# Transposed, mean-centred x for a cross-attention block: read from DRAM in a second layout instead of transposed on TensorE

## The chip, the cores and the metric

The kernel runs on one core of one Trainium2 chip, as a single launch. The metric is device time in microseconds (us) of one execution; several executions are timed and the median is given. The profile is one further execution taken by the hardware profiler. Engines are named as in the profile: PE is TensorE's matmul side, PEld its weight loads, DVE is VectorE, ACT is ScalarE, POOL is GpSimd, SP is SyncE, which here issues nearly all DMAs.

## The reference, cut to what matters

```python
def _layernorm(x, axis=-1, eps=1e-05):
    m = jnp.mean(x, axis=axis, keepdims=True)
    v = jnp.var(x, axis=axis, keepdims=True)
    return (x - m) / jnp.sqrt(v + eps)
...
# x (8, 128, 512), ctx_4096 (8, 128, 512), 32 heads of 128, 8 KV heads
q = (query @ Wq).reshape(nb, q_len, H, D).transpose(0, 2, 1, 3)
k = (key @ Wk).reshape(nb, q_len, KVH, D).transpose(0, 2, 1, 3)
v = (value @ Wv).reshape(nb, q_len, KVH, D).transpose(0, 2, 1, 3)
q = q * cos + _rotate_half(q) * sin
k = k * cos + _rotate_half(k) * sin
scores = jnp.einsum('bhqd,bhkd->bhqk', q, k) / jnp.sqrt(jnp.float32(D))
scores = jnp.where(mask == 0, jnp.float32(-1000000000.0), scores)
attn = jax.nn.softmax(scores, axis=-1)
...
x = x + _L0_xattn_ref(_layernorm(x, axis=-1), ctx_4096, ctx_4096, pos_BxS2, mask_BxSxS2_ik0, ...)
x = x + _L0_ffn_ref(_layernorm(x, axis=-1), ...)
```

The query of the attention is the layer norm of x. Each row of x is centred and multiplied by one number, 1/sqrt(var + eps). The projection by Wq and the rotation are linear, so that number can be applied before the projection or to the row's scores. The router block behind it is not touched by the change.

## The kernel before, in words

Five instruction streams are written out by hand, one for each engine, each in the fixed order of the code. They meet only through semaphores: an instruction waits until a semaphore has reached a count, and whatever is written behind it on its engine waits with it. There are 1024 rows of x and of the context (8 batches of 128), 512 columns, 8 KV heads. Every fp32 product is made of three products of split operands: a tensor is copied by ACT to a rounded part (names with `_hi`) and DVE or POOL subtracts that from the original to get the rest (`_lo`).

The stages, in the order in which PE works through them:

- Values, 16 tiles (i = 0 to 15; U_V + i in the code): PE projects the context by Wv into four PSUM banks in turn (bank_a, bank_b, outp0, bank_c). `copy_values(i)`, on DVE for i < 10 and on ACT for i from 10 on, copies tile i to `v_stage` (6 slots); SP stores it to DRAM (`store_v(i)`). PE needs the copy of tile u - 4 before it starts tile u. `copy_values(i)` for i >= 6 needs the store of tile i - 6 to have landed.
- Around tiles 8 to 11 the layer-normed x is made: `normalise_x(j)` on DVE, four 128x128 transposes on PE in `transpose_x(j)`, `copy_x(j)` on ACT into `x_raw`. Each of the eight j is one batch; with four of them half of the columns (q = 0) are ready, with eight the other half (q = 1).
- POOL then makes four sums of the blocks of `x_raw` (`sum_x(0)`, `sum_x(1)`: four instructions each, for a Strassen-like product of seven block products). ACT rounds all seven blocks (`hi_x(i, q)`, three of them from `x_raw` as it stands, four from the sums) and DVE makes the rests (`lo_x(i, q)`). I call this the x chain. Interleaved with it on ACT are `copy_values(10)` to `copy_values(15)` and `hi_wk(0)` to `hi_wk(5)`, and on DVE `lo_wk(0)` to `lo_wk(5)`; SP loads wk tile r + 2 when `lo_wk(r)` is done.
- Keys, 16 tiles (k = 0 to 15): PE projects the context by Wk; ACT copies the swapped halves, POOL multiplies by sin, DVE by cos and adds. Key tile k needs the copy of the tile four before it, so tile 2 needs `copy_values(14)` and tile 3 `copy_values(15)`.
- Then the first queries, and the main loop over KV heads and batches (scores, softmax, values, output projection, with the next queries in between), and the router block.

SP's DMAs all go to one hardware queue, in the order of its code.

Of the kernel before, what the change touches and what calls it, by code (L numbers as in the profile page):

```python
# [18 lines left out]
F32 = mybir.dt.float32  # L19
# [13 lines left out]
SCALE = float(D) ** -0.5  # L33


# [29 lines left out]
X_AFTER = 8  # L65
X_ORDER = 0, 4, 1, 5, 2, 6, 3, 7
# [15 lines left out]
def xattn_ffn(nc, x, ctx, pos, mask, rope, wq, wk, wv, wo, router, router_bias, expert_bias, out):  # L82
    v_dram = nc.dram_tensor("v_dram", (KV * NH * P, HB * D), F32, kind="Internal").ap()
    k_dram = nc.dram_tensor("k_dram", (KV * P, T), F32, kind="Internal").ap()
    with ExitStack() as stack:
# [20 lines left out]
        kT = at("kT", [T], F32, 82)  # L106
        hold = at("hold", [5, W], F32, 86)
# [72 lines left out]
        x_norm = at("x_norm", [2, E], F32, 194)  # L180
# [11 lines left out]
        x_rstd = at("x_rstd", [B], F32, 206.90625)  # L192
# [28 lines left out]
        x_bank = [probT, attnT]  # L221
# [28 lines left out]
        rstd_done = sem("rstd_done")  # L250
        norm_done = sem("norm_done")
# [6 lines left out]
        x_ps = sem("x_ps")  # L258
        x_copied = sem("x_copied")
# [137 lines left out]
        def _(sp):  # L397
# [35 lines left out]

            v_tiles = v_dram.rearrange("(g n p) (b d) -> n b p g d", g=KV, n=NH, d=D)
# [45 lines left out]
            sp.wait_ge(x_ps, B)  # L480
# [57 lines left out]
        def _(pool):  # L538
# [66 lines left out]
            pool.tensor_tensor(x_rstd[:, :], x_var[:, :], power[:, :], ALU.pow).then_inc(rstd_done, 1)  # L605
# [18 lines left out]
            pool.wait_ge(mask_done, 1)  # L624
            sum_x(0)
# [194 lines left out]
        def _(act):  # L820
# [90 lines left out]
            def copy_x(j):  # L911
                act.wait_ge(x_ps, j + 1)
                b = X_ORDER[j]
                half, rows = b // HB, slice(b % HB * S, (b % HB + 1) * S)
                act.activation(x_raw[:, 2 * half:2 * half + 2, :, rows],
                               x_bank[j % 2][:, :].rearrange("p (a c k) -> p a c k", a=2, c=HALVES), ACT.Copy).then_inc(x_copied, 1)
# [28 lines left out]
            copy_x(0)  # L945
            copy_x(1)
# [4 lines left out]
            copy_x(2)  # L951
            copy_x(3)
            for i in (B11, B21, B22):
                hi_x(i, 0)
            copy_x(4)
            copy_x(5)
# [3 lines left out]
            copy_x(6)  # L960
            copy_x(7)
# [284 lines left out]
        def _(dve):  # L1246
# [38 lines left out]
            def normalise_x(j):  # L1285

                b = X_ORDER[j]
                if j >= 2:
                    dve.wait_ge(x_ps, j - 1)
                dve.tensor_scalar(x_norm[:, j % 2, :], resid[:, b, :], x_mv[:, b, 0:1], x_rstd[:, b:b + 1],  # L1290
                                  ALU.subtract, ALU.mult).then_inc(norm_done, 1)
# [17 lines left out]
            for i in range(V_ACT):  # L1309
                copy_values(i)  # L1310
                if i in (3, 5):
                    half = 0 if i == 3 else 1
                    dve.wait_ge(dma_x[half], 16)
                    for b in range(half * HB, (half + 1) * HB):
                        dve.bn_stats(x_stats[:, b, :], resid[:, b, :]).then_inc(x_counted, 1)
                if i == 5:
                    dve.wait_ge(x_counted, B)
                    for b in range(B):
                        dve.bn_aggr(x_mv[:, b, :], x_stats[:, b, :]).then_inc(x_averaged, 1)
                    dve.wait_ge(x_averaged, B)  # L1320
                    dve.tensor_scalar(x_var[:, :], x_mv[:, :, 1], EPS, None, ALU.add).then_inc(var_done, 1)
# [898 lines left out]
```

## Time and profile before

| | before |
|---|---|
| median of 3 runs | 585.93 us (585.85 to 588.29) |
| span of the profiled execution | 584.1 us |
| PE busy | 577.0 us, 99% of the span |
| DVE / ACT / POOL busy | 471.4 / 404.1 / 430.9 us |
| DMA moved | 45.39 MB |

The profiled execution's span runs from its first instruction to its last. Its own time is that span and what lies around it, about 1.8 us by the median of the runs (585.93 - 584.1). Times inside the profile count from the start of the span. In a row of a timeline the first number is the start, the second the time for the xN instructions in it, and a bracket names the idle time ahead and what ended it.

### The profile page before, as it was taken

The numbers are of one execution on the slowest core, as the hardware profiler recorded it, in microseconds if no ns is written. First come the engines' busy times: TensorE is split into PE (matmuls) and PEld (weight loads), VectorE is DVE, ScalarE is ACT, GpSimd is POOL, SyncE is SP. The second block draws the span as 40 slices with busy tenths as digits, with TensorE's granted clock in tenths as the row PEclk, the third lists the DMA queues.
The fourth block names the chain that finished last, engine by engine and source line by source line (L and its number), as shares of the span: only waits on it lengthen the run. The fifth ranks groups of instructions, "written<-read, shape, count | busy, mean of one in ns | idle before, by whom it ended". The sixth has DMA issues, their size and how long they took to land.

```text
span 584.1 us, 10617 instructions
## 1 busy us (share of the span) xinstructions
PE 577.0 (99%) x2999; PEld 489.5 (84%) x2999; DVE 471.4 (81%) x764; ACT 404.1 (69%) x1074; POOL 430.9 (74%) x404
## 2 busy tenths in 40 slices
PE   9999999999999999999999999999999999999997
PEld 7888888877888888888888888888888888888885
DVE  5779797799888779777987798779877986797986
ACT  6267654797777777777776777677776776586655
POOL 5477699698976878687868886888678865446554
PEclk9999999999999999999999999999999999999999
DMA  8963526112301310121012110311122011100002
GB/s 287 378 182 91 160 93 227 38 38 90 109 20 54 91 56 19 55 90 54 24 48 90 54 49 23 90 54 54 36 72 63 8 50 59 36 20 2 19 37 91
DMA packets 30960, 45.39 MB, mean 78 GB/s; under 512 B 3024, under 2 KB 11600, under 8 KB 30928
## 3 DMA queue, kind: packets, MB, share of 16 engines
q1 hardware_dynamic: 30112, 43.56, 23.4%
q0 software_dynamic: 384, 1.05, 0.5%
q10 hardware_dynamic: 432, 0.40, 0.2%
q8 instruction: 15, 0.25, 0.2%
q14 instruction: 17, 0.14, 0.1%
HBM read 35.03 MB, written 9.96 MB: 77 GB/s over the span
## 4 chain that ended last, share of the span: by engine, by line
PE 92%; DVE 3%; ACT 2%; issue 2%; POOL 1%; DVEq 0%; ACTq 0%
PE score L1885 9%; PE outp L1909 9%; PE outp L1913 9%; PE outp L1917 8%; PE bank_a L1757 5%; PE bank_a L1759 5%; PE bank_a L1758 5%; PE probT L1964 4%; PE attnT L1743 2%; PE attnT L1744 2%; PE attnT L1745 2%; PE bank_c L1759 2%; PE bank_c L1758 2%; PE bank_c L1757 2%; PE bank_a L1743 1%
## 5 line engine op out<-in xcount | busy, mean ns | idle before, releaser
L543 POOL TENSOR_TENSOR rot<-rot,sinT 128x512 f32<-128x512 f32 x75 | 103.1, 1375 | 44.9 <-ACT rot L827 44.9
L1002 ACT ACTIVATE probs<-score,negmax 128x128 f32<-128x128 f32 x256 | 90.7, 366 | 28.7 <-DVE negmax L1412 28.7
L661 POOL TENSOR_TENSOR probs<-probs,rsum 128x512 f32<-128x512 f32 x62 | 67.3, 1085 | 44.1 <-DVE rsum L1418 44.1
L1909 PE MATMUL outp<-wo_hi,oT_hi 128*128 128x512 f32 x240 | 94.9, 397 | 0.2 <-DVE wo_lo L1479 0.2
L1913 PE MATMUL outp<-wo_lo,oT_hi 128*128 128x512 f32 x240 | 93.4, 391 | 0.3 <-POOL wo_lo L548 0.3
L1917 PE MATMUL outp<-wo_hi,oT_lo 128*128 128x512 f32 x240 | 83.4, 389 | 0.0
L1425 DVE TENSOR_TENSOR resid<-resid,outp 128x512 f32<-128x512 f32 x60 | 41.0, 683 | 48.8 <-PE outp L1917 46.9
L1885 PEld LDWEIGHTS score<-kT,qT 128*128 128x128 f32 x512 | 66.8, 191 | 5.0
L1254 DVE TENSOR_TENSOR qT<-qT,rot 128x512 f32<-128x512 f32 x57 | 68.5, 1205 | 2.9 <-POOL rot L543 0.5
L1129 ACT ACTIVATE oT_hi<-attnT 128x512 fp32r<-128x512 f32 x64 | 38.1, 595 | 42.9 <-PE attnT L1745 41.7
L1011 ACT ACTIVATE pT_hi<-probT 128x512 fp32r<-128x512 f32 x64 | 38.4, 600 | 42.4 <-PE probT L1964 41.8
L1885 PE MATMUL score<-kT,qT 128*128 128x128 f32 x512 | 67.4, 274 | 0.0
L1437 DVE TENSOR_TENSOR oT_lo<-attnT,oT_hi 128x512 fp32r<-128x512 f32 x64 | 44.2, 690 | 14.4 <-ACT oT_hi L1129 14.4
L548 POOL TENSOR_TENSOR wo_lo<-ring_b,wo_hi 128x512 fp32r<-128x512 f32 x30 | 38.7, 1322 | 21.6 <-ACT wo_hi L885 21.6
L1909 PEld LDWEIGHTS outp<-wo_hi,oT_hi 128*128 128x128 f32 x240 | 45.0, 188 | 10.4 <-DVE wo_lo L1479 1.1
L1917 PEld LDWEIGHTS outp<-wo_hi,oT_lo 128*128 128x128 f32 x240 | 45.1, 188 | 10.0
L1913 PEld LDWEIGHTS outp<-wo_lo,oT_hi 128*128 128x128 f32 x240 | 45.1, 188 | 9.9 <-POOL wo_lo L548 0.7
L1757 PE MATMUL bank_a<-x_hi,w_hi 128*128 128x512 f32 x120 | 51.9, 432 | 0.0
L1002 ACT ACTIVATION_READ_ACCUMULATOR probs<-score,negmax 128x1 f32 x256 | 51.9, 203 | 0.0
L1404 DVE SCALAR_TENSOR_TENSOR score<-score,mask_bias 128x512 f32<-128x512 f32 x64 | 44.5, 695 | 6.3 <-PE score L1885 3.0
L1759 PE MATMUL bank_a<-x_hi,w_lo 128*128 128x512 f32 x120 | 47.3, 394 | 0.0
L1758 PE MATMUL bank_a<-x_lo,w_hi 128*128 128x512 f32 x120 | 47.0, 391 | 0.0
(366 smaller groups left out, 1531.0 us busy)
## 6 DMA issues: line engine op xcount, KB each, us to landing
ring_b<-in_wo SPq DMA_DIRECT2D x32, 256.0 KB, 3.0
ring_a<-in_wq SPq DMA_DIRECT2D x28, 256.0 KB, 2.8
v_dram<-v_stage SPq DMA_DIRECT2D x16, 256.0 KB, 4.2
v_raw<-v_dram SPq DMA_DIRECT2D x16, 256.0 KB, 2.6
k_dram<-k_stage SPq DMA_DIRECT2D x14, 256.0 KB, 2.1
kT<-k_dram SPq DMA_DIRECT2D x14, 256.0 KB, 2.7
ctx_in<-in_ctx SPq DMA_DIRECT2D x8, 256.0 KB, 6.4
ring_b<-in_wv SPq DMA_DIRECT2D x8, 256.0 KB, 8.0
```

What stands on the lines that cost most here:

```text
L543: pool.tensor_tensor(rot_of(k0), rot_of(k0), sinT[:, half * W:(half + 1) * W], ALU.mult).then_inc(sin_done, 1)
L661: pool.tensor_tensor(probs[:, p], probs[:, p], rsum[:, p, :].unsqueeze(2).broadcast_to([P, GH, S]), ALU.mult).then_inc(soft_done, 1)
L1002: last = act.activation(probs[:, p, h, :], heads(score[p][:, :])[:, h, :], ACT.Exp, bias=negmax[:, p, h:h + 1], accum_out=sums[:, p, h:h + 1])
L1254: dve.tensor_tensor(dst, src, rot_of(k), ALU.add).then_inc(rope_done, 1)
L1404: dve.scalar_tensor_tensor(heads(score[p][:, :]), heads(score[p][:, :]), SCALE, mask_bias[:, b, :].unsqueeze(1).broadcast_to([P, GH, S]), ...
L1757: pe.matmul(ps[:, :], w[0], m[0], start=start and c == 0, stop=False, skip_group_check=True)
L1758: pe.matmul(ps[:, :], w[0], m[1], start=False, stop=False, skip_group_check=True)
L1759: last = pe.matmul(ps[:, :], w[1], m[0], start=False, stop=stop and c == HALVES - 1, skip_group_check=True)
L1885: last = pe.matmul(score[p][:, h * S:(h + 1) * S], qT[:, half, h, b % HB * S:(b % HB + 1) * S], kT[:, b * S:(b + 1) * S], start=True, stop ...
L1909: pe.matmul(ps[:, :], oT_hi[:, cols], wo_hi[:, h, :], start=h == 0, stop=False)
L1913: return pe.matmul(ps[:, :], oT_hi[:, cols], wo_lo[:, h, :], start=False, stop=stop)
L1917: return pe.matmul(ps[:, :], oT_lo[:, cols], wo_hi[:, h, :], start=False, stop=stop)
```

## The change

Four things change, all in the first stage.

1. The kernel gets a second input, `xt`, x laid out with the 512 columns as rows. SP loads it straight into `x_raw` in four DMAs of 512 KB. The 32 transposes of `transpose_x`, the eight `copy_x` and the eight `normalise_x` go.
2. The means lie one to a partition, but in `x_raw` they must lie along the free axis. SP writes them to DRAM (`store_mean(half)`: 512 elements of 4 bytes, one element to a run) and reads them back into all 128 partitions (`load_mean(half)`: 256 KB into `x_mean`). DVE subtracts them in place in `centre_x(q, half)`, four instructions of 128x1024. `x_mean` lies where kT is written later.
3. 1/sqrt(var + eps) is made together with 1/sqrt(128) as `score_scale`, and the instruction that scales and masks the scores takes it as a scalar for each partition instead of a constant.
4. The mask's load moves ahead of the wk loads, and the wait for `x_ps` ahead of the first wo loads goes.

```diff
             load_x(1)
+            sp.dma_start(mask_in[:, :, :], mask).then_inc(dma_mask, 16)
+            load_xt(0)
+            load_xt(1)
             for r in range(RA):
                 load_wk(r)
-            sp.dma_start(mask_in[:, :, :], mask).then_inc(dma_mask, 16)
             for i in range(KB * B):
+                if i == 6:
+                    store_mean(1)
                 store_v(i)
+                if i == 3:
+                    store_mean(0)
+                if i == 5:
+                    load_mean(0)
+                if i == 7:
+                    load_mean(1)
...
+            def load_xt(half):
+                cols = slice(half * W, (half + 1) * W)
+                for a in range(2):
+                    sp.dma_start(x_raw[:, 2 * half + a, :, :],
+                                 xt[a * HE:(a + 1) * HE, cols].rearrange("(c p) k -> p c k", p=P)).then_inc(dma_xt[half], 16)
+            def store_mean(half):
+                sp.wait_ge(x_averaged, (half + 1) * HB)
+                row = mean_dram[0, half * W:(half + 1) * W].rearrange("(b s) -> s b", s=S)
+                sp.dma_start(row, x_mv[:, half * HB:(half + 1) * HB, 0],
+                             allow_slow_non_contiguous=True).then_inc(dma_mout[half], 16)
+            def load_mean(half):
+                cols = slice(half * W, (half + 1) * W)
+                sp.wait_ge(dma_mout[half], 16)
+                sp.dma_start(x_mean[:, cols], mean_dram[:, cols].broadcast_to([P, W])).then_inc(dma_mean[half], 16)
...
+            def centre_x(q, half):
+                if q == 0:
+                    dve.wait_ge(dma_xt[half], 32)
+                    dve.wait_ge(dma_mean[half], 16)
+                rows = slice(q * 2 * S, (q + 1) * 2 * S)
+                block = x_raw[:, 2 * half:2 * half + 2, :, rows].rearrange("p a c k -> p (a c) k")
+                mean = x_mean[:, half * W + q * 2 * S:half * W + (q + 1) * 2 * S].unsqueeze(1).broadcast_to([P, 2 * HALVES, 2 * S])
+                dve.tensor_tensor(block, block, mean, ALU.subtract).then_inc(x_centred, 1)
...
-                if i == X_AFTER - 1:
-                    dve.wait_ge(rstd_done, 1)
-                    dve.wait_ge(b_lo, KB * C)
-                if i >= X_AFTER - 1:
-                    normalise_x(2 * (i - X_AFTER + 1))
-                    normalise_x(2 * (i - X_AFTER + 1) + 1)
+                if i == 7:
+                    centre_x(0, 0)
+                if i == 8:
+                    centre_x(0, 1)
+            centre_x(1, 0)
+            centre_x(1, 1)
             lo_wk(0)
-            normalise_x(6)
-            normalise_x(7)
...
             def sum_x(q):
-                pool.wait_ge(x_copied, (q + 1) * HB)
+                pool.wait_ge(x_centred, NH * (q + 1))
...
             def hi_x(i, q):
-                    act.wait_ge(x_copied, (q + 1) * HB)
+                    act.wait_ge(x_centred, NH * (q + 1))
...
             def mask_scores(p, b, count):
-                dve.scalar_tensor_tensor(heads(score[p][:, :]), heads(score[p][:, :]), SCALE,
+                dve.scalar_tensor_tensor(heads(score[p][:, :]), heads(score[p][:, :]), score_scale[:, b:b + 1],
...
-                if X_AFTER <= i < X_AFTER + HB:
-                    transpose_x(2 * (i - X_AFTER))
-                    transpose_x(2 * (i - X_AFTER) + 1)
```

SP's stream from the second load of x to the eighth value store, before (resid is x by rows, early_pair are the first Wq tiles):

```order
L432 DMA resid<-in_x 128x4x512
L406 DMA ring_a<-in_wk 128x512 x2
L468 DMA mask_in<-in_mask 128x1024
L439 DMA v_dram<-v_stage 128x4x128 [waits proj_free] x3
L417 DMA early_pair_61<-in_wq 128x512 x2
L439 DMA v_dram<-v_stage 128x4x128 [waits proj_free] x4
L417 DMA early_pair_60<-in_wq 128x512 [waits b_lo]
L417 DMA early_pair_60<-in_wq 128x512
L439 DMA v_dram<-v_stage 128x4x128 [waits proj_free] x3
```

The same stretch of SP's stream in the changed kernel:

```order
L428 DMA resid<-in_x 128x4x512
L480 DMA mask_in<-in_mask 128x1024
L433 DMA x_raw<-in_xt 128x2x512 x4
L402 DMA ring_a<-in_wk 128x512 x2
L453 DMA v_dram<-v_stage 128x4x128 [waits proj_free] x3
L413 DMA early_pair_62<-in_wq 128x512 x2
L453 DMA v_dram<-v_stage 128x4x128 [waits proj_free]
L440 DMA mean_dram<-x_mv 128x4x1 [waits x_averaged]
L453 DMA v_dram<-v_stage 128x4x128 [waits proj_free] x2
L446 DMA x_mean<-mean_dram 128x512 [waits dma_mout0]
L440 DMA mean_dram<-x_mv 128x4x1 [waits x_averaged]
L453 DMA v_dram<-v_stage 128x4x128 [waits proj_free]
```

Four 512 KB loads now stand ahead of the wk loads and all value stores. Two waits for a mean to have landed in DRAM stand in the stream, the first shown here, and the second mean's store stands behind the first wait.

DVE's stream from value tile 6 on, before:

```order
L1283 COPY v_stage<-outp 128x512 [waits dma_vout0,proj_done]
L1324 TENSOR_SCALAR mask_bias<-mask_in 128x1024 [waits dma_mask]
L1283 COPY v_stage<-bank_c 128x512 [waits dma_vout1,proj_done]
L1290 TENSOR_SCALAR x_norm<-resid,x_mv,x_rstd 128x512 [waits b_lo,rstd_done]
L1290 TENSOR_SCALAR x_norm<-resid,x_mv,x_rstd 128x512
L1283 COPY v_stage<-bank_a 128x512 [waits dma_vout2,proj_done]
L1290 TENSOR_SCALAR x_norm<-resid,x_mv,x_rstd 128x512 [waits x_ps] x2
L1283 COPY v_stage<-bank_b 128x512 [waits dma_vout3,proj_done]
L1290 TENSOR_SCALAR x_norm<-resid,x_mv,x_rstd 128x512 [waits x_ps] x2
```

The same stretch of DVE's stream in the changed kernel:

```order
L1292 COPY v_stage<-outp 128x512 [waits dma_vout0,proj_done]
L1335 TENSOR_SCALAR mask_bias<-mask_in 128x1024 [waits dma_mask]
L1292 COPY v_stage<-bank_c 128x512 [waits dma_vout1,proj_done]
L1302 TENSOR_TENSOR x_raw<-x_raw,x_mean 128x4x256 [waits dma_mean0,dma_xt0]
L1292 COPY v_stage<-bank_a 128x512 [waits dma_vout2,proj_done]
L1302 TENSOR_TENSOR x_raw<-x_raw,x_mean 128x4x256 [waits dma_mean1,dma_xt1]
L1292 COPY v_stage<-bank_b 128x512 [waits dma_vout3,proj_done]
L1302 TENSOR_TENSOR x_raw<-x_raw,x_mean 128x4x256 x2
L1306 TENSOR_TENSOR wk_lo<-ring_a,wk_hi 128x512 [waits k_hi] x2
```

The copies of value tiles 8 and 9 now stand behind waits for DMAs, where they stood behind work of PE.

## Rows read from the trace of the kernel before

**Rows 1.** The page: span, busy time by engine, 40 slices.
```profile
span 584.1 us, 10617 instructions
PE 577.0 (99%) x2999; PEld 489.5 (84%) x2999; DVE 471.4 (81%) x764; ACT 404.1 (69%) x1074; POOL 430.9 (74%) x404
...
DMA  8963526112301310121012110311122011100002
```

**Rows 2.** Timeline of PE: value tiles and transposes, then key tiles.
```profile
30.39 0.47 PE L1743 MATMUL bank_a<-wv_hi,ctxT_hi 128*128 128x512 f32 x1
...
33.24 0.60 PE L1844 MATMUL probT<-ident,x_norm 128*128 128x128 f32 x4
...
44.91 0.47 PE L1743 MATMUL bank_a<-wv_hi,ctxT_hi 128*128 128x512 f32 x1
...
47.76 0.39 PE L1743 MATMUL bank_b<-wv_hi,ctxT_hi 128*128 128x512 f32 x1
...
50.48 0.39 PE L1743 MATMUL outp<-wv_hi,ctxT_hi 128*128 128x512 f32 x1
...
64.08 0.39 PE L1743 MATMUL bank_c<-ctxT_hi,wk_hi 128*128 128x512 f32 x1
```

**Rows 3.** DMA by windows 23:30, 17:23 and 26.3:27; issues: KB, us to landing.
```profile
DMA packets 2869, 2.62 MB, mean 374 GB/s; under 512 B 142, under 2 KB 2253, under 8 KB 2868
...
v_dram<-v_stage SPq DMA_DIRECT2D x3, 256.0 KB, 11.0
...
v_dram<-v_stage SPq DMA_DIRECT2D x1, 256.0 KB, 5.8
```

**Rows 4.** Timeline of SP: when the DMAs were issued.
```profile
17.61 0.40 SPq L439 DMA_DIRECT2D v_dram<-v_stage  x1
...
26.36 0.98 SPq L439 DMA_DIRECT2D v_dram<-v_stage  x1
```

**Rows 5.** DMA issues up to 110 us: KB each, median us to landing.
```profile
ring_a<-in_wk SPq DMA_DIRECT2D x8, 256.0 KB, 2.9
...
rbias<-in_router_bias SPq DMA_DIRECT2D x1, 32.0 KB, 4.4
pos_in<-in_pos ACTq DMA_DIRECT2D x1, 4.0 KB, 2.9
```

**Rows 6.** Timeline of DVE.
```profile
28.80 0.69 DVE L1283 COPY v_stage<-outp 128x512 f32<-128x512 f32 x1
...
37.67 1.45 DVE L1290 TENSOR_SCALAR x_norm<-resid,x_mv,x_rstd 128x512 f32<-128x512 f32 x2
39.03 1.78 DVE L1295 TENSOR_TENSOR wk_lo<-ring_a,wk_hi 128x512 fp32r<-128x512 f32 x1
41.14 2.54 DVE L1290 TENSOR_SCALAR x_norm<-resid,x_mv,x_rstd 128x512 f32<-128x512 f32 x2 [0.33 <-PE probT L1844]
...
60.91 0.68 DVE L1295 TENSOR_TENSOR wk_lo<-ring_a,wk_hi 128x512 fp32r<-128x512 f32 x1
```

**Rows 7.** Timeline of ACT.
```profile
37.99 0.59 ACT L915 ACTIVATE x_raw<-attnT 128x512 f32<-128x512 f32 x1
...
55.06 2.20 ACT L925 ACTIVATE x_hi<-x_raw 128x512 fp32r<-128x512 f32 x4 [3.08 <-POOL x_raw L621]
...
57.68 0.58 ACT L942 ACTIVATE v_stage<-outp 128x512 f32<-128x512 f32 x1
60.17 0.63 ACT L909 ACTIVATE wk_hi<-ring_a 128x512 fp32r<-128x512 f32 x1 [1.91 <-DMA ring_a<-in_wk]
60.71 0.58 ACT L942 ACTIVATE v_stage<-bank_c 128x512 f32<-128x512 f32 x1
```

**Rows 8.** Timeline of POOL.
```profile
38.79 1.48 POOL L616 TENSOR_TENSOR x_raw<-x_raw 128x512 f32<-128x512 f32 x1
```

**Rows 9.** The page's costliest groups (busy us, mean ns), and one line's instructions (ns min/median/max).
```profile
L1404 DVE SCALAR_TENSOR_TENSOR score<-score,mask_bias 128x512 f32<-128x512 f32 x64 | 44.5, 695 | 6.3 <-PE score L1885 3.0
...
L1705 DVE SCALAR_TENSOR_TENSOR ff_out<-bank_a,ff_rsum,ff_y x1: 750/750/750, 579.2 to 579.2; 128x512 f32<-128x512 f32 x1
```

More of the change, by code:

```diff
@@ L32 @@
 EPS = 1e-5
-SCALE = float(D) ** -0.5
 MASKED = -(2.0**100)
@@ L64 @@
 TABLE_AFTER = 5, 7
-X_AFTER = 8
-X_ORDER = 0, 4, 1, 5, 2, 6, 3, 7
 WARM = 10
@@ L79, with xattn_ffn @@
 KEEP = 4, 1
-def xattn_ffn(nc, x, ctx, pos, mask, rope, wq, wk, wv, wo, router, router_bias, expert_bias, out):
+def xattn_ffn(nc, x, xt, ctx, pos, mask, rope, wq, wk, wv, wo, router, router_bias, expert_bias, out):
     v_dram = nc.dram_tensor("v_dram", (KV * NH * P, HB * D), F32, kind="Internal").ap()
     k_dram = nc.dram_tensor("k_dram", (KV * P, T), F32, kind="Internal").ap()
+    mean_dram = nc.dram_tensor("mean_dram", (1, T), F32, kind="Internal").ap()
     with ExitStack() as stack:
@@ L106, in xattn_ffn @@
         kT = at("kT", [T], F32, 82)
+        x_mean = at("x_mean", [T], F32, 82)
         hold = at("hold", [5, W], F32, 86)
@@ L191, in xattn_ffn @@
         x_var = at("x_var", [B], F32, 206.875)
-        x_rstd = at("x_rstd", [B], F32, 206.90625)
+        score_scale = at("score_scale", [B], F32, 206.90625)
         power = at("power", [B], F32, 206.9375)
@@ L249, in xattn_ffn @@
         var_done = sem("var_done")
-        rstd_done = sem("rstd_done")
-        norm_done = sem("norm_done")
+        scale_done = sem("scale_done")
+        dma_xt = [sem(f"dma_xt{i}") for i in range(NH)]
+        dma_mout = [sem(f"dma_mout{i}") for i in range(NH)]
+        dma_mean = [sem(f"dma_mean{i}") for i in range(NH)]
+        x_centred = sem("x_centred")
         mask_done = sem("mask_done")
@@ L604, in _ @@
             pool.wait_ge(var_done, 1)
-            pool.tensor_tensor(x_rstd[:, :], x_var[:, :], power[:, :], ALU.pow).then_inc(rstd_done, 1)
+            pool.tensor_tensor(score_scale[:, :], x_var[:, :], power[:, :], ALU.pow).then_inc(scale_done, 1)
             sums12(1, 0)
@@ L624, in _ @@
             pool.wait_ge(mask_done, 1)
+            pool.wait_ge(table_ps, 2 * NH)
             sum_x(0)
@@ L909, in hi_wk @@
                 act.activation(wk_hi[r % WK][:, :, :], chunks(ring_a[:, r % RA, :]), ACT.Copy).then_inc(k_hi, 1)
[L911 to L916, printed above, removed]
             def hi_x(i, q):
@@ L944, in _ @@
             act.wait_ge(proj_done, U_V + B)
-            copy_x(0)
-            copy_x(1)
             hi_wk(0)
@@ L1315, in _ @@
                         dve.bn_stats(x_stats[:, b, :], resid[:, b, :]).then_inc(x_counted, 1)
+                    dve.wait_ge(x_counted, (half + 1) * HB)
+                    for b in range(half * HB, (half + 1) * HB):
+                        dve.bn_aggr(x_mv[:, b, :], x_stats[:, b, :]).then_inc(x_averaged, 1)
                 if i == 5:
-                    dve.wait_ge(x_counted, B)
-                    for b in range(B):
-                        dve.bn_aggr(x_mv[:, b, :], x_stats[:, b, :]).then_inc(x_averaged, 1)
                     dve.wait_ge(x_averaged, B)
-                    dve.tensor_scalar(x_var[:, :], x_mv[:, :, 1], EPS, None, ALU.add).then_inc(var_done, 1)
+                    dve.tensor_scalar(x_var[:, :], x_mv[:, :, 1], EPS, float(D), ALU.add, ALU.mult).then_inc(var_done, 1)
                 if i == 6:
@@ L1443, in _ @@
             stored(0)
+            dve.wait_ge(scale_done, 1)
             make_c11(0, 0)
@@ L1835, in _ @@
                         last.then_inc(proj_done, 1)
-            def transpose_x(j):
-                pe.wait_ge(norm_done, j + 1)
-                if j == 0:
-                    pe.wait_ge(table_done, 2 * NH)
-                if j >= 2:
-                    pe.wait_ge(x_copied, j - 1)
-                for c in range(C):
-                    last = pe.transpose(x_bank[j % 2][:, c * P:(c + 1) * P], x_norm[:, j % 2, c * P:(c + 1) * P], ident[:, :])
-                last.then_inc(x_ps, 1)
             for i in range(len(early_banks), KB * B):
@@ L2073, in _ @@
             m1(1, 0, U_K + KK - 1)
-            pe.wait_ge(x_copied, B)
+            pe.wait_ge(table_done, 2 * NH)
             m2(1, 0)
@@ L2201 @@
         "x": x,
+        "xt": np.asarray(x).reshape(T, E).T,
         "ctx": np.asarray(ctx_4096).reshape(T, E).T,
```

17 lines of the change are left out of this document (removed).

## The prediction

> **What bounds the kernel now.** I read the page first. PE is busy 99% of the span, and DVE, the next, 81% [rows 1]. So time is won only where PE gets less to do, and lost only where PE is made to wait. The row of DMA in 40 slices shows the one other full resource: the first two slices, up to 29 us, stand at 8 and 9 tenths [rows 1], and the change adds transfers just there. Then I read the timelines of the first 65 us engine by engine, since all that changes lies in them, and looked in each for two things: how long PE spends on what goes, and how late the x chain may become before PE waits for it.
>
> **What is removed.** In the timeline of PE the value tile that starts at 30.39 and the three behind it are each followed by eight transposes; the tile after the fourth group starts at 44.91. So a tile with transposes takes (44.91 - 30.39) / 4 = 3.63 us. Without them a tile takes 50.48 - 47.76 = 2.72 us [rows 2]. Four times the difference is 3.64 us, the whole gain on PE. The eight copies on ACT (0.5 to 0.6 us) and the eight subtractions on DVE go too, but neither engine is the bound there except through the x chain, in which I count them below.
>
> **What is added to the queue.** The transposed x is four loads of 512 KB, 2.1 MB. The queue runs full at 374 GB/s between 23 and 30 us [rows 3], so they take 2.1 MB / 0.374 = 5.6 us, and nothing hides them. The backlog is seen in the landings: the three value stores issued from 17.61 us on take 11.0 us to land (median), the store issued at 26.36 us takes 5.8, so it lands at 32.2 [rows 3, 4]. All that is issued behind the new loads lands 5.6 us later. For most of it that costs nothing: the copy of value tile 6, which ran at 28.80 [rows 6], needs the first store, landed at 17.61 + 11.0 = 28.6; it now lands at 34.2. PE needs that copy at its tile 10, which without transposes starts at 36.0 (tile 8 takes 47.76 - 44.91 = 2.85 us, since transposes of another tensor precede it, tile 9 takes 2.72). The copy's 0.69 us just fit; a cover of 1.1 us is left.
>
> **The way of the means.** This is the new wait. The first mean's store stands behind the fourth value store, which lands at 32.2 + 5.6 = 37.8. No row has a DMA of 4-byte elements. The nearest are pos_in, 4 KB in small packets, 2.9 us from issue to landing with the queue empty, and rbias, 4.4 us [rows 5]. Behind a store that is itself waiting, part of that latency is covered, so I take 1.5 us past the fourth store: 39.3 (bounds 37.8 and 42.2, all or none of it covered). SP waits for it, then issues the load: 256 KB at 2.9 us [rows 5], and up to 1 us more because two value stores stand ahead. The mean lands at about 42.5.
>
> The second mean's store is issued only after the first load, at 39.7 or so, and lands 2.9 to 4.4 us later; I take 3.5: 43.2. SP waits again, behind one value store, two Wq loads and another value store that it has issued meanwhile, 1 MB or 2.8 us. The second load takes 2.9 us by itself and up to 1.2 more behind these: 47 us. With both means at their quickest (37.8 + 2.9 + 0.5 + 2.9 + 2.9, overlapping by what is already queued) I get 44.5; with both at 4.4 and the queue in full, 51.
>
> The Trainium skill, DMA: Bandwidth & Descriptors, section on the anatomy of one DMA, gives each DMA a fixed cost of about 2.0 us plus its bytes at 436 GB/s, so 2.0 us for a store of means and 2.6 for a load: the second mean would land at 37.8 + 2.6 + 0.4 + 2.0 + 2.6 = 45.4, and the sum below would come out 1.6 us lower. The trace has 2.9 us for the load [rows 5]; its specifications say that pieces under 512 bytes are read, modified and written, which no row here prices.
>
> **What waits for them.** On DVE the first `centre_x` waits until 42.5, the copy of value tile 8 behind it until 43.8, and PE, which would start tile 12 at 41.4, waits for it about 3 us. The second `centre_x` ends at 47 + 1.2 = 48.2 (twice the elements that take 0.68 us where POOL is idle [rows 6], less what two instructions would spend on starting twice; an estimate). Only then may POOL start its sums. Before, the fourth copy of x ended at 37.99 + 0.59 = 38.6 and POOL started at 38.79 [rows 7, 8]. The x chain is 48.2 - 38.6 = 9.6 us late.
>
> How much of that reaches PE? ACT waits 3.08 us for the last sum, then copies value tile 14 until 58.26 and value tile 15 until 60.71 + 0.58 = 61.29, the latter behind a wk load that waited for DVE [rows 7]. PE needs them at key tiles 2 and 3. Tile 3 starts at 64.08 [rows 2], tile 2 one tile earlier at 61.36. So the slack is 3.1 and 2.8 us, and 9.6 - 2.8 = 6.8 us reach PE.
>
> DVE has its own arm: from 37.67 on it is busy almost without a gap, to its sixth wk rest, which ends at 60.91 + 0.68 [rows 6]. Behind the 48.2 of now stand one copy and two more `centre_x` in place of the last subtractions (2.54 us and the 0.33 before them). POOL's sums run at the same time, and DVE's 512 elements then take 1.78 instead of 0.68 us [rows 6]. So the two cost 1.2 to 3.5 us each, 0.6 + 2.4 to 7.0 in place of some 3.4 (with the end of the pair of 37.67): between 0.4 us less and 4.2 us more. I take 1.5 more.
>
> Sum at key tile 3: 9.6 - 2.8 + 1.5 = 8.3 us later than before. PE's 3.64 us are already in it, because this start is no longer set by PE's own work. From there on PE works key tile after key tile as before, and everything behind is shifted by the same amount.
>
> **The rest.** The score instruction with a scalar for each partition: 64 of them take 695 ns now with a constant; the one with such a scalar took 750 [rows 9], so 0 to 64 x 0.055 = 3.5 us of DVE work. DVE is idle a fifth of the span while PE is full, so I take 0; if all of it were on the path it would be 3.5. The moved mask load, the aggregation in two parts and the dropped wait of the wo loads touch nothing that is waited for: 0.
>
> 584.1 + 8.3 = 592.4 us of span, with the 1.8 us around it 594.2. The median of the runs before, 585.9, already has the same 1.8, so this is 8.3 us or 1.4% slower.
>
> **Rivals.**
> - *The gain arrives.* PE keeps all 3.64 us if the x chain, with its slack of 2.8 us, runs 3.64 - 2.8 = 0.8 us ahead of its old time: 585.9 - 3.6 = 582.3. For it speaks that all added work is off PE; against it that SP must be past 37.8 us before even the first mean's store can land. It needs the new loads not to push the queue (5.6 us less) and quick means. The second mean must land before 38.6 - 0.8 - 1.2 = 36.6 us for the full gain, before 38.6 + 2.8 - 1.2 = 40.2 for any. Chance 0.12.
> - *A draw.* The second mean lands at 40 to 43, DVE's arm costs nothing, and the waits eat the gain: 38.6 + 2.8 - 1.2 is 40.2, so up to 2.8 us late, 586 to 588.7. It needs the mean stores to land before the value stores ahead of them. Chance 0.12.
> - *The means are slower than any row:* 4-byte elements into DRAM take 6 us or more each. Both lie in series, so the x chain is another 5 us later than I have it, or more: from 594.2 + 5 = 599 to 605. Chance 0.16.
> - *My forecast,* second mean at 43 to 50 us: 588.7 (no cost on DVE's arm) to 597.2 (1.5 us, 50 + 1.2 - 38.6 - 2.8 + 1.5 = 11.3). Chance 0.60.
>
> **How the numbers follow.** The time is the likeliest, 594.2. The range takes in the bounds of the means (44.5 to 51) and of DVE's arm (-0.4 to +4.2): 9.6 can be 7.1 or 13.6, so the shift is 7.1 - 2.8 - 0.4 = 3.9 to 13.6 - 2.8 + 4.2 = 15.0; 589.8 to 600.9. To leave out no more than 2 in 10 it reaches down into the draw and up into the slow means: 585.5 to 602. About 0.5%, 2.9 us, is what can be told from no change here. Faster by more than that 0.12, within 0.12, slower 0.76.
>
> **What would show it.** Right: in the timeline of DVE a wait of several us for `x_mean` in front of the first two `centre_x`, PE's waits for `v_stage` at value tiles 12, 13 and 15, POOL's first sum at about 48, key tile 3 near 72. Wrong: POOL's first sum before 42, or the value stores landing no later than before, or a main loop in which PE waits for the masked scores. If the granted clock fell during PE's waits, the time would be longer than I say.

## The result and the profile after

The changed kernel takes 607.92 us (median of 4 runs, 607.63 to 608.38) against 585.89 us (4 runs, 585.51 to 588.29): a ratio of 1.0376, 95% interval 1.0361 to 1.0391. That is slower, as forecast, but by 22.0 us where 8.3 were forecast, and outside the range.

The page of the profiled execution, with the rows that answer to [rows 1], and those of PE and of its granted clock in 40 slices:

```profile
span 605.7 us, 10543 instructions
PE 579.0 (96%) x2967; PEld 488.1 (81%) x2967; DVE 474.7 (78%) x760; ACT 399.7 (66%) x1066; POOL 433.2 (72%) x404
...
PE   9973799999999999999999999999999999999997
...
PEclk9995899999999999999999999999999999999999
DMA  8997451610230121102212121310121002010002
```

One slice is 15.1 us. PE loses time in the third to fifth slice, 30 to 76 us, and nowhere else that the slices show. Where, the waits of PE up to 140 us say (us in total, times, longest):

```profile
PE bank_a L1753 <- DVE v_stage L1292: 14.4, 2, 14.2
PE bank_c L1753 <- ACT v_stage L959: 3.3, 1, 3.3
...
PE outp L1767 <- ACT part_u L886: 0.7, 1, 0.7
PE outp L1753 <- ACT v_stage L959: 0.7, 1, 0.7
PE bank_a L1767 <- ACT part_t L880: 0.5, 1, 0.5
```

The first is value tile 12, which waits for DVE's copy of tile 8; the forecast had 3 us there. Why DVE was late stands in its timeline, which answers to [rows 6]:

```profile
33.70 0.69 DVE L1292 COPY v_stage<-outp 128x512 f32<-128x512 f32 x1 [5.57 <-DMA v_dram<-v_stage]
...
53.48 1.23 DVE L1302 TENSOR_TENSOR x_raw<-x_raw,x_mean 128x1024 f32<-128x1024 f32 x1 [17.88 <-DMA x_mean<-mean_dram]
...
57.93 1.23 DVE L1302 TENSOR_TENSOR x_raw<-x_raw,x_mean 128x1024 f32<-128x1024 f32 x1 [2.63 <-DMA x_mean<-mean_dram]
...
59.67 4.26 DVE L1302 TENSOR_TENSOR x_raw<-x_raw,x_mean 128x1024 f32<-128x1024 f32 x2
```

The copy of value tile 6 starts where the forecast put it (34.2). Then DVE stands still for 17.9 us for the first mean. SP's timeline has the two stores and the two loads of means, and answers to [rows 4]; each of the last three rows starts when what it waited for had landed, or right behind the one above it:

```profile
32.22 1.00 SPq L440 DMA_DIRECT2D mean_dram<-x_mv  x1
...
43.52 0.34 SPq L446 DMA_DIRECT2D x_mean<-mean_dram  x1
43.90 0.43 SPq L440 DMA_DIRECT2D mean_dram<-x_mv  x1
...
54.30 0.33 SPq L446 DMA_DIRECT2D x_mean<-mean_dram  x1
```

The first store was issued at 32.22 and awaited until 43.52, 11.3 us; the second took 43.90 to 54.30, 10.4 us. The first load, issued just ahead of the second store, landed only at 53.4, when DVE went on: 9.9 us for what takes 2.9 in [rows 5]. The second load took 3.6 us (54.30 to 57.93). The issues between 30 and 70 us (KB each, median us to landing):

```profile
v_dram<-v_stage SPq DMA_DIRECT2D x9, 256.0 KB, 10.2
early_pair<-in_wq SPq DMA_DIRECT2D x4, 256.0 KB, 7.4
x_mean<-mean_dram SPq DMA_DIRECT2D x2, 256.0 KB, 6.7
...
mean_dram<-x_mv SPq DMA_DIRECT2D x2, 2.0 KB, 10.8
```

Whatever shares the queue with a mean's store is slow with it: in the kernel before, the nine value stores of the same stretch took 3.1 us (median). The windows (busy time by engine, then the granted clock, the DMA share and GB/s) show how:

```profile
30.00:42.00 12.00, 11.19 (x51) 8.97 (x49) 1.89 (x3) 3.15 (x6) 4.82 (x6) 1.00 1.15 198
...
34.00:42.00 8.00, 7.19 (x32) 5.63 (x30) 1.59 (x3) 0.94 (x2) 4.82 (x6) 1.00 1.17 113
42.00:56.00 14.00, 0.64 (x2) 0.55 (x3) 1.83 (x2) 0.00 (x0) 0.00 (x0) 0.55 0.80 108
56.00:62.00 6.00, 6.00 (x19) 4.74 (x18) 4.07 (x4) 2.81 (x6) 2.60 (x2) 0.62 0.41 109
```

From 34 to 56 us the DMA engines count as busy (1.17 and 0.80) while they move 110 GB/s, against 374 in [rows 3]. The lateness goes two ways from there: down the x chain, to POOL's first sum (38.79 before [rows 8]) and on to PE's key tile 3 (64.08 before [rows 2]), and through the copy of value tile 8 to PE's tile 12:

```profile
59.32 1.29 POOL L639 TENSOR_TENSOR x_raw<-x_raw 128x512 f32<-128x512 f32 x1 [17.93 <-DVE x_raw L1302]
...
55.36 0.79 PE L1753 MATMUL bank_a<-wv_hi,ctxT_hi 128*128 128x512 f32 x1 [14.16 <-DVE v_stage L1292]
...
83.33 0.50 PE L1753 MATMUL bank_c<-ctxT_hi,wk_hi 128*128 128x512 f32 x1
```

### The profile page after: what moved, and what is told of

Its sections match the earlier page's. It is cut to its first block, busy times and chain, and to the rows that moved or that the text cites. A ratio compares the mean times of both kernels' runs of the same rounds, so it can differ in the third digit from the quotient of the medians.

```text
span 605.7 us, 10543 instructions
## 1 busy us (share of the span) xinstructions
PE 579.0 (96%) x2967; PEld 488.1 (81%) x2967; DVE 474.7 (78%) x760; ACT 399.7 (66%) x1066; POOL 433.2 (72%) x404
## 4 chain that ended last, share of the span: by engine, by line
PE 73%; DVE 7%; DMA 5%; POOL 5%; issue 5%; ACT 3%; SPq 2%; DVEq 0%; ACTq 0%; POOLq 0%
PE score L1882 9%; PE outp L1906 8%; PE outp L1910 8%; PE outp L1914 8%; PE bank_a L1767 4%; PE bank_a L1769 4%; PE probT L1961 4%; PE bank_a L1768 4%; DMA mean_dram<-x_mv 4%; PE attnT L1753 2%; PE attnT L1755 2%; PE attnT L1754 2%; PE bank_c L1769 2%; PE bank_c L1768 2%; PE bank_c L1767 2%
## 5 line engine op out<-in xcount | busy, mean ns | idle before, releaser
L1906 PEld LDWEIGHTS outp<-wo_hi,oT_hi 128*128 128x128 f32 x240 | 45.0, 188 | 10.7 <-DVE wo_lo L1489 1.1
L1413 DVE SCALAR_TENSOR_TENSOR score<-score,score_scale,mask_bias 128x512 f32<-128x512 f32 x64 | 48.3, 755 | 5.9 <-PE score L1882 2.4
```

The lines of the kernel that those rows point to most:

```text
L1413: dve.scalar_tensor_tensor(heads(score[p][:, :]), heads(score[p][:, :]), score_scale[:, b:b + 1], mask_bias[:, b, :].unsqueeze(1).broadcas ...
L1906: pe.matmul(ps[:, :], oT_hi[:, cols], wo_hi[:, h, :], start=h == 0, stop=False)
```

## Experiments

Three theories for the 22 us. A: each packet of 4 bytes holds its DMA engine some 250 ns, so a store of 512 holds the queue 8 us. B: the loss is the 2.1 MB of transposed x ahead of everything. C: a store to DRAM that is waited for and read back costs some 10 us whatever its packets. Each time stands against the kernel before on the same chip (585.6 to 586.0 us).

**Stores alone.** The kernel before, with the two stores of means added, unread.

```diff
+                if i == 6:
+                    store_mean(1)
                 store_v(i)
+                if i == 3:
+                    store_mean(0)
...
```

> The kernel before with the two mean stores alone added at their new places in SP's queue, unread and waited for by nobody, without the transposed x. Theory A (a 4-byte packet holds a DMA engine for about 250 ns, so a store of 512 of them, 32 to an engine, holds the queue for 8 us by itself): the stores take 8 to 10 us from issue to landing here too, the value stores behind them land some 8 us later than before, and the time is 585 to 588, since the copies that need those slots have 8 us of room. Theory B (the stores are late only because 2 MB of transposed x stand ahead): 3 to 5 us to landing, time 585.9. Theory C (a store that is read back at once takes 10 us): nothing is read back here, so 3 to 5 us.

586.49 us, ratio 1.0017 (1.0007 to 1.0026). With no load of x ahead and nobody waiting, the stores still took 13.5 and 16.0 us to land, more than A's 8 to 10. So their latency is neither B's nor C's. It cost the kernel next to nothing, because nothing was waiting: the price is paid only by who waits.

**No stores.** The changed kernel without the two stores, with `x_mean` loaded from an input row, without a wait. The means are left out of its result.

```diff
-                sp.wait_ge(dma_mout[half], 16)
-                sp.dma_start(x_mean[:, cols], mean_dram[:, cols].broadcast_to([P, W])).then_inc(dma_mean[half], 16)
+                sp.dma_start(x_mean[:, cols], xt[0:1, cols].broadcast_to([P, W])).then_inc(dma_mean[half], 16)
...
-                if i == 6:
-                    store_mean(1)
                 store_v(i)
-                if i == 3:
-                    store_mean(0)
```

> The changed kernel without the two mean stores: the loads of the means read the first row of the transposed input instead, at the same places in the queue and waiting for nothing; DVE subtracts that row. The means are left out of the result; all else stands, the 2 MB of transposed x too. Theory A and theory C (the store is the loss): POOL's first sum starts at 38 to 42, the time is 583 to 587, at least 20 us below the changed kernel. Theory B (the loads of transposed x are the loss): still 595 or more.

592.78 us, ratio 1.0122 (1.0105 to 1.0138), POOL's first sum at 44.02. The stores and their waits are 15 of the 22 us. No theory had the other 7; they are taken up below.

**Stores twice.** Each store of means preceded by a twin into a tensor that nobody reads.

```diff
+                twin = twin_dram[0, half * W:(half + 1) * W].rearrange("(b s) -> s b", s=S)
+                sp.dma_start(twin, x_mv[:, half * HB:(half + 1) * HB, 0],
+                             allow_slow_non_contiguous=True).then_inc(dma_twin[half], 16)
                 row = mean_dram[0, half * W:(half + 1) * W].rearrange("(b s) -> s b", s=S)
```

> The changed kernel with each mean store issued twice, first to a DRAM tensor that nobody reads. Theory A (the packets cost): each twin holds the queue 8 us more, so the second mean is 16 us later and the time is 620 to 628. Theory B and theory C (queue ahead, or a fixed round trip): the twin adds at most 1 us each, 608 to 610.

609.59 us, ratio 1.0407 (1.0382 to 1.0433): 1.7 us more than the changed kernel where A wants 8 for each twin. The issues between 30 and 70 us:

```profile
twin_dram<-x_mv SPq DMA_DIRECT2D x2, 2.0 KB, 10.7
mean_dram<-x_mv SPq DMA_DIRECT2D x2, 2.0 KB, 10.1
```

Twice the packets land in the same time. A falls as I had put it: the price does not go by packets. Two stores into different rows run side by side.

**Means stored as rows.** PE transposes the means to 4 partitions, ACT copies them out of PSUM, and the store has 4 packets of 512 bytes; load, waits and places stay.

```diff
...
-                sp.dma_start(row, x_mv[:, half * HB:(half + 1) * HB, 0],
-                             allow_slow_non_contiguous=True).then_inc(dma_mout[half], 16)
...
+                sp.dma_start(row, mean_row[:, half, :]).then_inc(dma_mout[half], 16)
```

> The changed kernel with the means turned into rows first: PE transposes the four means of a half to 4x128, ACT copies them, and the store has 4 packets of 512 bytes in place of 512 of 4. The round trip through DRAM and both waits stay. Theory A: a store lands in 2 to 4 us, POOL's first sum starts at 43 to 48, the time is 588 to 595, which is what the prediction counted with. Theory C: a store still takes 8 us or more, 603 to 608. Theory B: 595 to 608, since the transposed x stays ahead of it.

594.47 us, ratio 1.0146 (1.0129 to 1.0163). SP's timeline:

```profile
32.32 0.45 SPq L443 DMA_DIRECT2D mean_dram<-mean_row  x1
...
36.66 0.34 SPq L448 DMA_DIRECT2D x_mean<-mean_dram  x1
37.05 0.33 SPq L443 DMA_DIRECT2D mean_dram<-mean_row  x1
...
39.56 0.44 SPq L448 DMA_DIRECT2D x_mean<-mean_dram  x1
```

The same round trip through DRAM, with the same wait, takes 4.3 and 2.5 us. C falls: it is the form of the store.

**Prices in a quiet queue.** Four unread stores at about 104 us in the kernel before, each awaited before the next.

```diff
+            sp.dma_start(price_row[0, :].rearrange("(b s) -> s b", s=S), means,
+                         allow_slow_non_contiguous=True).then_inc(priced, 16)
+            sp.wait_ge(priced, 16)
+            sp.dma_start(price_far[:, 0].rearrange("(b s) -> s b", s=S), means,
+                         allow_slow_non_contiguous=True).then_inc(priced, 16)
...
```

> The kernel before, with four unread stores in a quiet stretch of the queue (about 104 us on), each waited for before the next: the 512 means of one half as elements of 4 bytes into one row of 2 KB; the same 512 elements, each 512 bytes from the next; 128 elements into 512 bytes; 512 elements with the four of each partition side by side. Theory 'crowd' (the 10 to 16 us of a mean store come from the busy queue and the value stores beside it): each lands in 2 to 4 us here. Theory 'packets' (each element costs its engine a fixed time): the three of 512 are equal, 8 us or more, that of 128 a third of it or less above a fixed 2 us. Theory 'lines' (writes into the same few lines of memory go one after another): the row takes 8 us or more, the spread one 2 to 4, the one of 128 in between.

```profile
price_row<-x_mv SPq DMA_DIRECT2D x1, 2.0 KB, 9.3
price_far<-x_mv SPq DMA_DIRECT2D x1, 2.0 KB, 1.8
price_one<-x_mv SPq DMA_DIRECT2D x1, 0.5 KB, 9.3
price_own<-x_mv SPq DMA_DIRECT2D x1, 2.0 KB, 7.1
```

The last column is us to landing. The same 512 packets take 9.3 us side by side and 1.8 us when they lie 512 bytes apart; a quarter of them, side by side, takes 9.3 again. So neither the crowd nor the packets, but neighbours in memory: 'lines' is the theory that is left, though its 128 did not come out in between. That kernel took 594.43 us in its one run: SP stood at the four stores from 104.48 to 131.89, and PE then waited 8.1 us for `probs`. Here too the price is paid by who waits. (The two kernels below, with shorter waits, took 585.40 and 585.39 us, one run each.)

**Prices by distance and by number.** Two more kernels of the same kind, with other distances and other counts.

> The kernel before, with four unread stores of 4-byte elements in the quiet stretch at 104 us, each waited for before the next: 512 elements 64 bytes apart, 512 elements 32 bytes apart, 512 elements 8 bytes apart, and 16 elements from 16 partitions side by side in 64 bytes. The row of 2 KB took 9.3 us, 128 elements in 512 bytes 9.3, 512 elements 512 bytes apart 1.8. Theory 'line of 64 bytes' (16 writes to one line go one after another at (9.3 - 1.8) / 15 = 0.5 us each, lines side by side): 1.8, 2.3, 5.3 and 9.3 us. Theory 'block of 512 bytes' (128 writes to one block, (9.3 - 1.8) / 127 = 0.06 us each): 2.2, 2.7, 5.5 and 2.7 us. So the 16 elements tell them apart.

> The kernel before, with four unread stores of 4-byte elements in the quiet stretch, each waited for before the next: 32 and then 64 elements side by side, 128 elements 8 bytes apart, 128 elements 64 bytes apart. So far, side by side: 16 elements 1.3 us, 128 elements 9.3 us, 512 elements 9.3 us; 512 elements 8 bytes apart 3.2, 32 bytes apart 1.9. Theory 'count' (within a few hundred bytes the price grows with the elements that lie side by side, (9.3 - 1.3) / 112 = 0.07 us each): 2.4 and 4.7 us, and the two of 128 that do not touch 3 us and 1.5 us. Rival 'step' (it is there or not, from some number of writers on): each of the first two is near 1.3 or near 9.3, nothing between.

The first, 512 elements 64, 32 and 8 bytes apart, and 16 side by side (one answer for each store); then the second, 32 and 64 side by side, 128 elements 8 and 64 bytes apart:

```profile
price<-x_mv SPq DMA_DIRECT2D x1, 2.0 KB, 2.7
...
price<-x_mv SPq DMA_DIRECT2D x1, 2.0 KB, 1.9
...
price<-x_mv SPq DMA_DIRECT2D x1, 2.0 KB, 3.2
...
price_few<-x_mv SPq DMA_DIRECT2D x1, 0.1 KB, 1.3
```

```profile
price_thirty<-x_mv SPq DMA_DIRECT2D x1, 0.1 KB, 4.7
price_sixty<-x_mv SPq DMA_DIRECT2D x1, 0.2 KB, 6.3
price_gap<-x_mv SPq DMA_DIRECT2D x1, 0.5 KB, 2.9
price_wide<-x_mv SPq DMA_DIRECT2D x1, 0.5 KB, 1.4
```

Sixteen neighbours in 64 bytes take 1.3 us, where a line of 64 bytes should have taken 9.3 and a block of 512 bytes 2.7: neither law is right. 'Count' was nearer than 'step': 1.3, 4.7, 6.3 and 9.3 us for 16, 32, 64 and 128 side by side, growing, but not by equal amounts (2.4 and 4.7 were expected for 32 and 64). The first store of each kernel holds part of a store of keys issued just ahead of it: the 4.7, the 2.7 and the 9.3 of the row (the 9.3 of 128 elements does not). A gap of 4 bytes between neighbours takes most of the price away. The rule behind it stays open.

**Spread in place.** The changed kernel with each element of a mean 512 bytes from the next.

```diff
-                row = mean_dram[0, half * W:(half + 1) * W].rearrange("(b s) -> s b", s=S)
+                row = mean_dram[half * W:(half + 1) * W, 0].rearrange("(b s) -> s b", s=S)
...
-                sp.dma_start(x_mean[:, cols], mean_dram[:, cols].broadcast_to([P, W])).then_inc(dma_mean[half], 16)
+                sp.dma_start(x_mean[:, cols], xt[0:1, cols].broadcast_to([P, W])).then_inc(dma_mean[half], 16)
```

> The changed kernel with one edit in place: each element of a mean store goes 512 bytes from the next in DRAM instead of side by side; same 512 packets, same places in the queue, same two waits. x_mean is then read from a row of the transposed x, so the means are left out of the result. Theory 'lines' (what a mean store costs is that its writes fall into the same few lines of memory, 9.3 us against 1.8 us in a quiet queue): both stores land in 3 to 5 us, POOL's first sum comes at 44 to 47, the time is 592 to 596, as with the means stored as four rows (594.5). Theory 'packets' or 'crowd' (512 packets beside value stores cost 10 us wherever they go): the stores stay at 9 to 11 us and the time above 604.

595.54 us, ratio 1.0163 (1.0143 to 1.0182). POOL's first sum and PE's key tile 3, and PE's waits up to 150 us:

```profile
47.72 1.29 POOL L639 TENSOR_TENSOR x_raw<-x_raw 128x512 f32<-128x512 f32 x1 [5.81 <-DVE x_raw L1302]
...
71.74 0.50 PE L1753 MATMUL bank_c<-ctxT_hi,wk_hi 128*128 128x512 f32 x1
```

```profile
PE bank_a L1753 <- DVE v_stage L1292: 3.0, 2, 2.8
PE bank_c L1753 <- ACT v_stage L959: 2.9, 1, 2.9
PE outp L1753 <- ACT v_stage L959: 2.3, 1, 2.3
...
```

The time is what 'lines' has; the first sum came 0.7 us later than its 44 to 47. The stores were awaited for 5.3 us (32.76 to 38.04) and 3.6 us (38.44 to 42.05), with as many packets in the same queue. So 12.4 of the 22 us go with the neighbours. The load of the means reads another tensor here, but that is not what it gains: the row form, which reads the means back, takes 594.5.

**Means spread on the chip.** No round trip: DVE multiplies the identity by the means, PE multiplies ones by that, and `centre_x` reads PSUM. Then the same with the loads of x behind the first three value stores and two Wq loads.

```diff
...
-                mean = x_mean[:, half * W + q * 2 * S:half * W + (q + 1) * 2 * S].unsqueeze(1).broadcast_to([P, 2 * HALVES, 2 * S])
+                mean = score[half][:, q * 2 * S:(q + 1) * 2 * S].unsqueeze(1).broadcast_to([P, 2 * HALVES, 2 * S])
...
+                    pe.matmul(score[i - 6][:, :], early_ones[:, :], diag[:, i - 6].rearrange("p b s -> p (b s)"),
+                              start=True, stop=True).then_inc(mean_ps, 1)
...
                 if i == 2:
                     load_pair(1, 0)
+                    load_xt(0)
+                    load_xt(1)
...
```

> The changed kernel with the means spread over the partitions on the chip: DVE multiplies the identity by the means, two matmuls of ones by that leave the broadcast means in two PSUM banks, and the subtractions read them there; no DRAM round trip at all, loads of transposed x where they were. Theory 'mean way': what the kernel without mean stores still lost (592.8 against 585.8) were the two loads of x_mean (5.3 us each) and their place in the queue: then POOL's first sum comes at 40 to 41 (38.79 before, 44.0 there), inside the slack of 2.8 us, PE keeps its 3.6 us less about 1.8 for the two new matmuls, and the time is 583 to 586. Rival 'backlog': the 2 MB of x ahead of the value stores hold back the copy of value tile 6 and with it all that DVE does behind it; then POOL's first sum stays at 43 to 44 and the time is 590 to 593.

> As the run before it, but the four loads of transposed x are issued behind the first three value stores and the first two Wq loads. Theory 'backlog': the copy of value tile 6 comes back to 29 us (33.3 to 33.7 in the kernels with the loads ahead), x lands at 33 and 36, POOL's first sum starts at 37 to 38.5, and PE keeps its gain less its two matmuls: 583 to 585, a draw or a little faster than before, and at least 3 us faster than the run before it if that is at 590. Rival 'mean way': place of the loads does not matter, both runs give the same time within 1 us. Rival 'DVE': POOL's and DVE's contention behind the first sum sets the time, and both stay above 588 with POOL's first sum below 39.

588.14 us, ratio 1.0045 (1.0028 to 1.0062), with POOL's first sum at 41.26; and 585.55 us, ratio 0.9988 (0.9975 to 1.0002), with the copy of tile 6 back at 29.24 and the first sum at 40.07. The first lies between its two theories. The place of the loads is worth 2.6 us, so the backlog counts, but 'backlog' had put the first run at 590 to 593 and the second at 583 to 585: x landed later than forecast (the first subtractions started at 36.07 and 38.68), and the time is a draw, not a gain. PE's waits in the second say where the gain is:

```profile
PE outp L1755 <- ACT part_u L868: 0.7, 1, 0.7
PE bank_a L1755 <- ACT part_t L862: 0.6, 1, 0.6
```

Its two matmuls of means stand in the trace as four of 0.59 us each, 2.4 in all; with these 1.3 us PE's 3.64 are gone.

**No centring.** The kernel with late loads, with neither means nor `centre_x`; POOL and ACT wait for the loads themselves.

```diff
-                pool.wait_ge(x_centred, NH * (q + 1))
+                pool.wait_ge(dma_xt[0], 32)
+                pool.wait_ge(dma_xt[1], 32)
...
```

> The kernel with transposed x loaded late, with the centring left out altogether (no spread of means, no subtraction; the means are not taken from x): what is left of the change is the transposes gone and the four loads added. It tells what PE's 3.64 us are worth once nothing on the means' way costs anything. Theory 'PE': they arrive in full, 585.8 - 3.6 = 582.2 (581.7 to 582.7), and PE waits for nothing in the value and key tiles. Rival 'key tiles': DVE, ACT and POOL, which are no faster than before in the key tiles, hold PE there (the 1.2 to 1.3 us for part_t and part_u that every changed kernel shows): then 583.0 to 584.0, with these two waits still there.

583.51 us, ratio 0.9962 (0.9949 to 0.9974): 2.1 us. 'Key tiles' holds. PE has 573.2 us of work instead of 577.0, so the transposes were 3.8, but the waits are still there:

```profile
PE outp L1735 <- ACT part_u L869: 0.7, 1, 0.7
PE bank_a L1735 <- ACT part_t L863: 0.6, 1, 0.6
```

PE is 4.0 us ahead of the kernel before at its first query matmul (95.42 against 99.44) and 2.2 behind the two waits (ACT's first `oT_hi`, 133.34 against 135.53), so they take 1.8 us, not only the 1.3 of their rows. Of the 4.0 this one execution had 1.25 already at value tile 8 (29.14 against 30.39), ahead of the first transpose of x, so the 4.0 is not the transposes alone.

**Cheaper means.** The late loads with the means as two bf16 parts, one pass each, and then these matmuls one tile later.

```diff
-                if i in (6, 7):
-                    pe.wait_ge(diag_done, 2 * (i - 5))
+                if i in (7, 8):
+                    pe.wait_ge(diag_done, 2 * (i - 6))
...
```

> The kernel with transposed x loaded late and the means spread on the chip, with the means split in two bf16 parts, so that each half takes two matmuls at one pass each instead of the four measured at 0.59 us for both halves (2.4 us of PE). If PE's own work now sets the time, as its waits in that run say (none left in the value tiles), the time falls by 0.7 to 1.5 us from 585.6, to 584 to 585, faster than before by 0.2 to 0.35%. Rival: what sets the time there is not PE but the key tiles' chain on DVE and POOL behind the first sum (part_t and part_u come 1.3 us late at the query tiles): then it stays at 585 to 586.

> The kernel with the means as two bf16 parts, with its matmuls one value tile later each. There PE waited 0.7 us for the second part of the first means, and the four matmuls took 0.38 us each. Sum of PE by rows: 3.64 less 4 x 0.38 = 1.5 less the 1.3 us for part_t and part_u leaves 0.8 us: 585.0 (584.6 to 585.4), 0.7 below the 585.7 or so of the run before it. Rival 'key tiles': the time stays at 585.6 to 586, since what PE saves ahead of the key tiles it waits for in them.

585.99 us, ratio 1.0004 (0.9995 to 1.0014), where PE now waited 0.7 us for the second part; and 585.52 us, ratio 1.0002 (0.9993 to 1.0012). Both miss their first expectation; the rivals were nearer. The second has one of its waits shorter (0.3 us for part_t) and a profiled span of 583.5 us against 584.1, though PE is 1.3 us ahead up to its last wait (578.14 against 579.42). The rest goes in the last store of the output, first before, then in this kernel (last column: us to landing):

```profile
out<-ff_end ACTq DMA_DIRECT2D x1, 128.0 KB, 2.4
...
out<-ff_end ACTq DMA_DIRECT2D x1, 128.0 KB, 3.2
```

It takes 3.3 us in the other kernel with bf16 parts and 2.4 in all others; why is open. The runs of the second reach from 584.53 to 587.61, so no gain can be told from them. No version with centring that I tried beats the kernel before.

## Why the prediction was right in sign and wrong in size

**The step that failed** is the price of a mean's store: "I take 1.5 us past the fourth store" and, for the second, "I take 3.5: 43.2". They took 11.3 and 10.4 us. Put at 39.3 and 43.2 us, the two landed at 43.52 and 54.30, 4.2 us later and then another 6.9, and these 11.1 us are all that the first sum came behind the forecast (59.32 against 48.2). I had taken pos_in and rbias [rows 5] as the nearest rows, but the first is 4 KB that go into the chip and the second is a load; neither writes neighbouring elements of 4 bytes into DRAM. With the elements 512 bytes apart the forecast comes out nearly: stores landed at 38.04 and 42.05 (forecast 39.3 and 43.2), first sum at 47.72 (about 48), PE's wait at tile 12 of 2.8 us (3), key tile 3 at 71.74 (near 72), 595.5 us (594.2). The row form gives 594.5.

The Trainium skill, DMA: Bandwidth & Descriptors, section on the anatomy of one DMA, has about 2.0 us fixed for a DMA of few bytes, measured on DMAs that GpSimd issues. These are issued by SyncE; the trace is near that figure for elements far apart (1.8 us) and far from it for neighbours (9.3 us). Its rules for kernel authors say that a strided last dimension becomes one descriptor for each element and should be rearranged: rows in place of elements saved 13.4 us here (607.9 to 594.5). But the number of packets is not the reason here: as many of them, far apart, save 12.4.

**The rival of slow means** was the right one, at 0.16, and still too low: "6 us or more each" gave 599 to 605, with 5 us more on the x chain where it was 11. The first load of a mean, 9.9 us beside the second store, is not in this: the second load was issued only when the second store had landed, at 54.30. The slow first load held the copy of tile 8 and so PE's tile 12, but PE waited again at tile 15.

**The queue** was right: the copy of tile 6 started at 33.70 (34.2), and the cover held.

**From the means to PE** was right. With the first sum 20.5 us late (59.32 - 38.79) instead of 9.6, the forecast's sum is 20.5 - 2.8 + 1.5 = 19.2; key tile 3 came 83.33 - 64.08 = 19.25 us later. This is more than one lucky sum: from the first sum to key tile 3 it was 25.3 us before, the forecast makes 25.3 - 2.8 + 1.5 = 24.0 of it, and the five kernels whose sum came at 44 us or later (this one, no stores, stores twice, rows, spread) show 24.0 to 24.1. PE's waits stand at tiles 12 and 15 and at key tile 2, not at tile 13.

**"Everything behind is shifted by the same amount"** was wrong by 21.6 - 19.25 = 2.4 us of span. Most of it is named. PE is 19.4 us late at its first query matmul (118.87 against 99.44), but DVE 21.8 at its first step behind the keys (`hold`, 125.05 against 103.28). So PE waits there for part_t and part_u, 0.5 and 0.7 us in its rows, and is 21.2 late behind them (ACT's first `oT_hi`, 156.73 against 135.53). These waits are in every kernel without the transposes. Another 0.4 us are lost between 506 and 527 us of the kernel before; that is open. So PE's 3.64 us, right as work, were worth 2.1 at most.

**The score's scalar** takes 755 ns where the constant took 695 [rows 9], 3.8 us of DVE in all. PE does not pay for it: by the starts of `oT_hi` the changed kernel is between 21.2 and 21.4 us late all through the main loop, from 135 to 506 us of the kernel before. So the 0 stands within 0.2 us.

**The clock** fell, as the last sentence feared: the granted clock is 0.55 in the mean from 42 to 56 us, at the lower of its two levels (1.2 GHz) for most of it, and tile 12 takes 60.58 - 55.36 = 5.2 us instead of 2.72. It did not lengthen the time, since PE waited again, 3.3 us at tile 15, for a copy that stands behind the x chain on ACT. The clock fell once more in tile 15 (0.67 in the mean from 69 to 74 us; the tile took 73.79 - 69.52 = 4.3 us), and that was covered too: PE waited 0.7 us at key tile 2, and key tile 3 started as soon as ACT's copy of value tile 15 was done (83.28). So this sign came, but not the longer time.

**Where the time went,** from run to run in this order (on the chips used the kernel before took 585.6 to 586.0 us, so some tenths mean nothing): 12.4 us neighbours (607.9 to 595.5), 2.8 the two awaited stores (to 592.8), 4.6 the loads of means and their place, net of PE's new matmuls (to 588.1), 2.6 the place of the loads of x (to 585.6), 2.0 the centring that was left (to 583.5). Of these 24.4 us 22.0 lie above the kernel before, and the rest is the gain that there was to be had.

## What to carry to other kernels

Before a value that lies one to a partition is sent through DRAM, ask in what form it is written: 128 or more elements of 4 bytes side by side took 9 to 16 us here and, in a busy queue, slowed all that shared it; a row or a spread took 2 to 5. A price for which no row stands should be bounded by a run of that operation, not by the nearest row that happens to exist. And an engine's saved work is worth only what the next chain has in slack: 3.64 us less on PE gave 2.1 at most.

## What had not been expected of the hardware

- 4-byte stores from different partitions into neighbouring addresses: 1.3, 4.7, 6.3 and 9.3 us for 16, 32, 64 and 128, and 9.3 for four times 128; 1.8 for 512 that lie 512 bytes apart. In the quiet queue the DMA engines are idle for most of the 9.3 us (share 0.08 from 106 to 108 us, 0.00 from there to 112); in the busy one they count as busy, at 110 GB/s.
- Two such stores into different rows run side by side (10.1 and 10.7 us), and a 256 KB load in the same queue takes 9.9 us instead of 2.9.
- While PE stood for 14 us the granted clock fell, and its next tile still ran at 1.2 instead of 2.4 GHz: matmuls start 0.43 instead of 0.23 us apart up to 60 us. Behind the wait of 3.3 us at tile 15 they start 0.23 apart at first, then 0.43 from 70.8 to 73.8 us.
